# One core, linear attention with a router: padded DRAM blocks of x, evenly spaced steps of the second half, a split load of finished tiles and another order in the tail

## The chip, the cores and the metric

The kernel runs on one core of one Trainium2 chip. The metric is the device time of one execution in microseconds (us). The kernel before took 1077.23 us as the median of three runs (1074.14 to 1080.42).

## The reference, cut to what matters

`x` is four sequences of 512 rows and 512 columns. Each row is normalised (`xn`), and two branches read `xn`:

```
s = attention(xn)      # 16 heads of 128: q, k, v = silu(xn @ w_qkv); causal linear attention with a
                       # decay per head; RMS norm over all heads times norm_w; times
                       # sigmoid(xn @ w_gate); times w_out
g = silu(router(xn))   # softmax over 64 experts, the 8 largest kept:
                       # xn * sum(weights) + weights @ expert_bias
out = x + s * g
```

All arrays are float32.

## The kernel before, in words

**Halves and heads.** The four sequences are handled as two halves of two. For each half the kernel goes through 8 pairs of heads, so there are 16 cycles (`CYC`), numbered c. A cycle has 28 slots (`SLOTS`), one for each large matrix product, and the slot number is the clock of the whole plan: `plan(s, f, ...)` puts a step into slot s, and the main loop (L1261 to L1273) issues one product and then the steps of that slot (`inserts`). Every engine has one instruction list, filled in this order, and takes it in order; so a waiting instruction holds back all that stands behind it on its engine. Waits are on semaphores that name a finished instruction (`tk[...]`).

**Products.** One cycle has four groups g = 4c + k (weights of v, of k and q, of the gates, of k and q). A group is a product of two block matrices in a seven-product form (`PROD`), with each operand split in a high and a low part (`XH`, `XL`, `WH`, `WL`), so a product is six matmuls of 128x512 (L162 to L164). The seven blocks of x, X11 to XT4, lie in `XH` and `XL`, 512 KB each in either. The order within the loop is 6, 2, 5, 7 of g, then 1 of g + 1, then 4 and 3 of g. Products 1 and 2 write `BA`, 5 and 3 `BD`, the others `BS`. After each, ACT and DVE read the bank out (L536 to L595), and the next writer waits for that: `bd_free` is set by the add of L551.

**Second half of x.** It is prepared during cycles 4 to 7. For each of four tiles of rows (`x_second`, L986) SP loads two tiles into `XR` 0 and 1, statistics and a norm follow, and then two units (kk = 0, 1): `unit_turn` transposes four 128x128 pieces on PE into `PX` and ACT copies them to `U`, which lies in `XR` 2 and 3 (L1010); POOL, ACT and DVE make the differences and the two parts; `unit_store` (L1037) writes both to DRAM, `dxh` and `dxl`, and frees `U` when the store has landed. `PX` is also the bank of the output products (`ypart`, L775), which stand in slots 10, 12, ... 24 of each cycle, and of the router. While group 31 runs, the last of the first half, each of its products frees one block, and `x_block` (L1044), issued from ACT right behind that product, loads the block's second half from DRAM. The first product of group 32 that reads a block waits for its load (L509).

**Turned heads.** `v_turn` and `k_turn` transpose 32x32 squares on DVE into `VB` or `P`, and `v_move` and `k_move` (L616, four DMAs each, from SP) bring them to their partitions. `VB` is one buffer: the next `v_turn` waits until the move has landed (`vb_free`).

**Finished tiles.** At the start of the second half the first half's eight output tiles are finished: `final_load` (L1174) loads the tile of x and the router's part (`dgd`) into two of the four `XR` buffers, `final_first` multiplies on DVE (L964) and adds on POOL (L968), `final_store` stores from SP (L1187). For the second half the same is done in the tail (L1276 to L1320), straight from eight banks: `final_last` multiplies on DVE (L974), adds on POOL or DVE (L977) and stores from SP (L979). `rms_in` (L900) makes the row factors `rr`: eight matmuls (L905), one DVE instruction (L912), one on POOL (L914).

Of the kernel before, what the change touches and what calls it, by code (L numbers as in the profile page):

```python
# [5 lines left out]
F32 = mybir.dt.float32  # L6
# [6 lines left out]
T = 512  # L13
# [4 lines left out]
C = 128  # L18
# [7 lines left out]
EARLY = 8  # L26
NXT = 4


X11, X21, X22, XT3, XT1, XT2, XT4 = range(7)  # L30

# [6 lines left out]
def build(nc, x, wp, small, rw, eb, out):  # L38

    with ExitStack() as ctx:  # L40
# [6 lines left out]
        def sem(name):  # L47
            return ctx.enter_context(nc.semaphore(name))

        dxh = nc.dram_tensor("dxh", (128, 14, T), F32, kind="Internal").ap()  # L50
        dxl = nc.dram_tensor("dxl", (128, 14, T), F32, kind="Internal").ap()
        dgd = nc.dram_tensor("dgd", (NB, T, H), F32, kind="Internal").ap()

        XH = sb("XH", [128, 14, T], F32R)
# [50 lines left out]
        PT = pb("PT")  # L105
# [40 lines left out]
        def dma(s, f, e="sp"):  # L146

            count[s.name] += 16
            prog[e].append(lambda eng: f(eng).then_inc(s, 16))
            return s, count[s.name]  # L150

        def wait(e, *tokens):
            for t in tokens:
                if t and t[1] > waited[e].get(t[0].name, 0):
                    waited[e][t[0].name] = t[1]
                    prog[e].append(lambda eng, t=t: eng.wait_ge(t[0], t[1]))

        def f32(ap):
            return ap.bitcast(F32)
# [109 lines left out]
        def x_tile(b, t, *more):  # L269

            k = xr_next[0] % NXT
            xr_next[0] += 1
            wait("sp", xr_free[k], *more)
            return XR[:, k, :], dma(s_x[k], lambda e: e.dma_start(XR[:, k, :], x[b, t * 128:(t + 1) * 128, :])), k
# [692 lines left out]
            wait("pool", a, xtok)  # L967
            return op("pool", lambda e: e.tensor_tensor(xa, xa, ga, ALU.add))  # L968

        def final_last(b, t, bank, xt, gt, s, en):  # L970

            (xa, xtok), (ga, gtok) = xt, gt
            wait("dve", gtok, tk["rr", b], tk["yl", b, t])
            tk["y_read", b, t] = a = op("dve", lambda e: e.scalar_tensor_tensor(  # L974
                ga, bank[:, :], rr[:, b, t:t + 1], ga, ALU.mult, ALU.mult))
            wait(en, a, xtok)
            a = op(en, lambda e: e.tensor_tensor(xa, xa, ga, ALU.add))  # L977
            wait("sp", a)
            return dma(s, lambda e: e.dma_start(out[2 + b, t * 128:(t + 1) * 128, :], xa))  # L979
# [55 lines left out]
            tk["ul"] = op("dve", lambda e: e.tensor_tensor(U.bitcast(F32R), U, f32(UH), ALU.subtract))  # L1035

        def unit_store(t, kk):  # L1037
            s = slice(t * 128, (t + 1) * 128)
            wait("sp", tk["uh"], tk["ul"])
            dma(s_us, lambda e: e.dma_start(dxh[:, kk::2, s], f32(UH)))  # L1040
            d = dma(s_us, lambda e: e.dma_start(dxl[:, kk::2, s], U))
            xr_free[2] = xr_free[3] = tk["uh_free"] = tk["us"] = d

        def x_block(i, free):  # L1044
            s = slice(2 * i, 2 * i + 2)
            wait("act", tk["us"], free)
            dma(s_xb[i], lambda e: e.dma_start(f32(XH[:, s, :]), dxh[:, s, :]), "act")
            tk["xb", i] = dma(s_xb[i], lambda e: e.dma_start(f32(XL[:, s, :]), dxl[:, s, :]), "act")

# [2 lines left out]
        def plan(s, f, *a):  # L1054
            at.setdefault(s, []).append((f, a))
# [103 lines left out]
        plan(2, router_loads)  # L1159
        plan(17, router_parts, 0)  # L1160
        plan(8, router_parts, 1)
        for t, (load, stats, norm, s0, s1) in enumerate(((119, 122, 125, 129, 139), (140, 143, 146, 149, 159),
                                                         (160, 163, 166, 169, 179), (180, 183, 186, 189, 199))):
            plan(load, x_second, t)
            plan(stats, x_second_stats, t)
            plan(norm, x_second_norm, t)
            for kk, s in enumerate((s0, s1)):
                at.setdefault(s, []).insert(0, (unit_turn, (t, kk)))
                for i, f in ((1, unit_mix), (2, unit_more), (4, unit_high), (5, unit_low), (6, unit_store)):
                    plan(s + i, f, t, kk)  # L1170
# [1 line left out]
        fin = {}  # L1172

        def final_load(b, t):  # L1174
            xt = x_tile(b, t)
            k = xr_next[0] % NXT
            xr_next[0] += 1
            fin[b, t] = (*xt, XR[:, k, :], g_load(0, b, t, XR[:, k, :], s_gl[k], xr_free[k]), k)

        def final_first(b, t):  # L1180
            xa, xtok, k, ga, gtok, kg = fin[b, t]
# [8 lines left out]
        plan(base + 11, rms, 0)  # L1190
        plan(base + 15, rms, 1)
        for i, (b, t) in enumerate((b, t) for b in range(2) for t in range(4)):
            plan(base + (13 if i < 2 else 15) + 3 * i, final_load, b, t)
            plan(base + 18 + 3 * i, final_first, b, t)
            plan(base + 20 + 3 * i, final_store, b, t)


        t0 = [(G[:, t // 2, t % 2, :], dma(s_xs[t], lambda e, t=t: e.dma_start(
# [81 lines left out]
        tail_load(7, lambda: (*tk["q_read", 0], tk["p_read", 0]), ST[:, 0:T], P[:, 0, :])  # L1280
        banks = (PX, BS[0], BA, PS, BS[1], BD, PO, PX)
        ends = []

        def halves(r, b, ts):
            for t in ts:
                ypart_half(c, r, b, t, banks[4 * b + t])

        def finals(i, en):
            ends.append(final_last(*divmod(i, 4), banks[i], *tails[i], s_to[i], en))

        seed(1, 0, BS[1], tk["bs_free", 1])
        inter(c, 1, 1)
# [15 lines left out]
        finals(0, "pool")  # L1308
        seed(1, 3, PX, tk["y_read", 0, 0])
        finals(1, "dve")  # L1310
        finals(2, "pool")
        finals(3, "dve")
        halves(0, 1, (0,))
        rms_in(1, PT, 16, (tk["rr", 0],))
        halves(0, 1, (1, 2, 3))
        halves(1, 1, range(4))
        finals(4, "pool")
        finals(5, "dve")
        finals(6, "pool")
        finals(7, "dve")  # L1320
        assert not at, at.keys()
        wait("sp", *ends)
        for i in range(NXT):
# [74 lines left out]
```

How the kernel before makes its waits and increments, by code:

```python
        def op(e, f):  # L139
            s = done[e]
            count[s.name] += 1
            prog[e].append(lambda eng: f(eng).then_inc(s, 1))
            return s, count[s.name]
# [1 line left out]
        def dma(s, f, e="sp"):  # L146
            count[s.name] += 16
            prog[e].append(lambda eng: f(eng).then_inc(s, 16))
            return s, count[s.name]
# [1 line left out]
        def wait(e, *tokens):  # L152
            for t in tokens:
                if t and t[1] > waited[e].get(t[0].name, 0):
                    waited[e][t[0].name] = t[1]
                    prog[e].append(lambda eng, t=t: eng.wait_ge(t[0], t[1]))
```

## Time and profile before

| | |
|---|---|
| median of 3 runs | 1077.23 us |
| the profiled execution's own time | 1076.92 us |
| its span | 1075.2 us |
| PE / PEld / DVE / ACT / POOL busy | 97 / 83 / 59 / 56 / 63 % |
| mean granted clock of TensorE | 0.993 of full |
| DMA, mean over the span | 105 GB/s |

PE is TensorE, PEld its weight loads, DVE VectorE, ACT ScalarE, POOL GpSimd; SPq and ACTq are DMA issues of SyncE and ScalarE. The profile's times start at the span's start; the run's time is 1.7 us longer than the span. Line numbers are those of the kernel before. In the DMA views q1 is the queue of SP and q10 that of ACT, and a packet is one run of adjacent bytes.

### The profile page before, as it was taken

The numbers are of one execution on the slowest core, as the hardware profiler recorded it, in microseconds if no ns is written. First come the engines' busy times: TensorE is split into PE (matmuls) and PEld (weight loads), VectorE is DVE, ScalarE is ACT, GpSimd is POOL, SyncE is SP. The second block draws the span as 40 slices with busy tenths as digits, with TensorE's granted clock in tenths as the row PEclk, the third lists the DMA queues.
The fourth block names the chain that finished last, engine by engine and source line by source line (L and its number), as shares of the span: only waits on it lengthen the run. The fifth ranks groups of instructions, "written<-read, shape, count | busy, mean of one in ns | idle before, by whom it ended". The sixth has DMA issues, their size and how long they took to land.

```text
span 1075.2 us, 15318 instructions
## 1 busy us (share of the span) xinstructions
PE 1045.3 (97%) x5540; PEld 889.4 (83%) x5540; DVE 632.7 (59%) x1047; ACT 600.5 (56%) x1074; POOL 672.2 (63%) x700
## 2 busy tenths in 40 slices
PE   7899999999999999999899989999999999999997
PEld 6688887888888887888788878888888888888886
DVE  5357556664756665556355565756666575555557
ACT  7666556564656655575455445646556465645543
POOL 6966556574766857586566775755657375665613
PEclk8999999999999999999999999999999999999999
DMA  4233223252434435345733652321334251332235
GB/s 152 77 82 83 52 63 93 67 148 70 128 98 128 122 102 154 94 108 145 283 101 94 186 162 47 86 64 46 94 97 121 67 159 48 74 94 59 63 94 183
DMA packets 214508, 112.59 MB, mean 105 GB/s; under 512 B 175520, under 2 KB 189984, under 8 KB 214432
## 3 DMA queue, kind: packets, MB, share of 16 engines
q1 hardware_dynamic: 198880, 59.68, 23.5%
q10 hardware_dynamic: 15552, 51.93, 15.1%
q8 instruction: 44, 0.72, 0.3%
q14 instruction: 32, 0.26, 0.1%
HBM read 66.47 MB, written 15.73 MB: 76 GB/s over the span
## 4 chain that ended last, share of the span: by engine, by line
PE 85%; DMA 4%; POOL 3%; ACT 3%; DVE 2%; SPq 1%; issue 1%; ACTq 0%; DVEq 0%; POOLq 0%
PE BS L162 7%; PE BS L164 7%; PE BS L163 7%; PE PX L162 5%; PE PX L163 5%; PE PX L164 5%; PE PS L643 5%; PE BD L162 5%; PE PO L728 5%; PE BA L162 5%; PE BD L164 5%; PE BA L164 5%; PE BD L163 5%; PE BA L163 5%; PE PT L692 4%; PE PO L712 4%
## 5 line engine op out<-in xcount | busy, mean ns | idle before, releaser
L480 POOL TENSOR_TENSOR WL<-ST,WH 128x768 fp32r<-128x768 f32 (+1 forms) x128 | 172.5, 1349 | 131.4 <-ACT WH L476 131.2
L480 POOL TENSOR_TENSOR WL<-STG,WH 128x512 fp32r<-128x512 f32 (+1 forms) x128 | 133.2, 1041 | 139.6 <-ACT WH L476 139.6
L162 PE MATMUL BS<-XH,WH 128*128 128x512 f32 x384 | 159.2, 415 | 3.1 <-ACT K L560 1.6
L164 PE MATMUL BS<-XH,WL 128*128 128x512 f32 x384 | 150.7, 392 | 0.0
L163 PE MATMUL BS<-XL,WH 128*128 128x512 f32 x384 | 150.0, 391 | 0.0
L793 DVE TENSOR_TENSOR Y<-Y,PX 128x512 f32<-128x512 f32 x104 | 71.4, 687 | 122.5 <-PE PX L164 122.0
L162 PE MATMUL BD<-XH,WH 128*128 128x512 f32 x256 | 104.2, 407 | 5.5 <-DVE K L551 5.3
L751 POOL TENSOR_TENSOR SS<-SS,SQ 128x512 f32<-128x512 f32 x60 | 86.6, 1444 | 31.7 <-ACT SQ L743 31.7
L162 PE MATMUL BA<-XH,WH 128*128 128x512 f32 x256 | 102.9, 402 | 0.0
L164 PE MATMUL BD<-XH,WL 128*128 128x512 f32 x256 | 100.7, 393 | 0.0
L163 PE MATMUL BD<-XL,WH 128*128 128x512 f32 x256 | 100.4, 392 | 0.0
L164 PE MATMUL BA<-XH,WL 128*128 128x512 f32 x256 | 100.1, 391 | 0.0
L163 PE MATMUL BA<-XL,WH 128*128 128x512 f32 x256 | 99.8, 390 | 0.0
L162 PE MATMUL PX<-OH,GH 128*128 128x512 f32 x244 | 97.1, 398 | 2.5 <-ACT XR L1010 1.7
L476 ACT ACTIVATE WH<-ST 128x768 fp32r<-128x768 f32 (+1 forms) x128 | 80.1, 626 | 30.5 <-PE BD L164 15.4
L163 PE MATMUL PX<-OL,GH 128*128 128x512 f32 x244 | 95.1, 390 | 0.0
L164 PE MATMUL PX<-OH,GL 128*128 128x512 f32 x244 | 95.1, 390 | 0.0
L162 PEld LDWEIGHTS BS<-XH,WH 128*128 128x128 f32 x384 | 72.4, 189 | 17.5 <-ACT K L560 2.9
L536 ACT ACTIVATE BS<-BA 128x512 f32<-128x512 f32 x64 | 37.2, 582 | 88.2 <-PE BA L164 88.2
L164 PEld LDWEIGHTS BS<-XH,WL 128*128 128x128 f32 x384 | 72.0, 188 | 16.3
L163 PEld LDWEIGHTS BS<-XL,WH 128*128 128x128 f32 x384 | 72.5, 189 | 12.1
L611 DVE STREAM_TRANSPOSE VB<-VT 128x512 f32<-128x512 f32 x64 | 69.4, 1084 | 8.6 <-DMA V<-VB 8.4
(303 smaller groups left out, 2405.8 us busy)
## 6 DMA issues: line engine op xcount, KB each, us to landing
STG<-in_wp ACTq DMA_DIRECT2D x77, 512.0 KB, 3.8
V<-VB SPq DMA_DIRECT2D x248, 64.0 KB, 2.4
KN<-P SPq DMA_DIRECT2D x240, 48.0 KB, 2.1
XR<-in_x SPq DMA_DIRECT2D x38, 256.0 KB, 3.2
dgd<-XR ACTq DMA_DIRECT2D x16, 256.0 KB, 2.8
dxh<-WT SPq DMA_DIRECT2D x8, 448.0 KB, 3.4
dxl<-XR SPq DMA_DIRECT2D x8, 448.0 KB, 4.3
XH<-dxh ACTq DMA_DIRECT2D x7, 512.0 KB, 6.0
```

The source lines that it names most:

```text
L162: eng.matmul(o, ah, bh, start=first, stop=False, skip_group_check=skip)
L163: eng.matmul(o, ah, bl_, start=False, stop=False, skip_group_check=skip)
L164: return eng.matmul(o, al, bh, start=False, stop=last, skip_group_check=skip)
L476: a = op("act", lambda e, dst=dst, src=src: e.activation(WH[:, u, dst], src, ACT.Copy))
L480: a = op("pool", lambda e, dst=dst, src=src: e.tensor_tensor(WL[:, u, dst], src, f32(WH[:, u, dst]), ALU.subtract))
L611: return op("dve", lambda e: e.transpose(to.rearrange("p (q k j) -> p q k j", q=4, k=n), src.rearrange("p (k i q) -> p q k i", k=n, q=4)))
L643: m = e.matmul(PS[:, chunk(k)], kk[:, chunk(k)], q[:, chunk(k)], start=(k == 0), stop=True, skip_group_check=True)
L692: m = e.matmul(PT[:, chunk(i)], KD[:, chunk(i)], v[:, i, :], start=True, stop=True)
L712: m = e.matmul(PO[:, chunk(k)], KV[:, k - 1, :], q[:, chunk(k)], start=(k == 1), stop=False, skip_group_check=True)
L728: m = e.matmul(PO[:, chunk(k)], v[:, k, :], P[:, b, chunk(k)], start=False, stop=True, skip_group_check=True)
L751: a = op("pool", lambda e: e.tensor_tensor(SS[:, b, :], SS[:, b, :], SQ[:, :], ALU.add))
L793: a = op("dve", lambda e: e.tensor_tensor(dst, dst, bank[:, :], ALU.add))
```

## The change

Four things are changed. `dxh` and `dxl` get a dimension of four tiles with 16 unused floats behind each 128, so that the 512 columns of a block are no longer adjacent in DRAM and `x_block` reads them as runs of 512 bytes; the stores write the same runs as before, at other addresses. The units of the second half start in slots 129 + 11n (n = 0 to 7) rather than 129, 139, 149, 159, 169, 179, 189, 199; their loads come 22 slots apart. For finished tiles the load of the router's part is issued 4 slots ahead of the multiply and the load of x 2 slots ahead, in place of both together 3 ahead (5 for the first two), and every second tile starts one slot later. In the tail the second row factor is computed ahead of the multiplies of tiles 2 and 3, the sum of tile 5 moves from DVE to POOL, that of tile 6 from POOL to DVE, and the sums of 6 and 7 come behind both multiplies.

```diff
--- before.py
+++ after.py
@@ -26,6 +26,8 @@
 EARLY = 8
 NXT = 4
 
+RUN = 16
+
 
 X11, X21, X22, XT3, XT1, XT2, XT4 = range(7)
 
@@ -47,8 +49,8 @@
         def sem(name):
             return ctx.enter_context(nc.semaphore(name))
 
-        dxh = nc.dram_tensor("dxh", (128, 14, T), F32, kind="Internal").ap()
-        dxl = nc.dram_tensor("dxl", (128, 14, T), F32, kind="Internal").ap()
+        dxh = nc.dram_tensor("dxh", (128, 14, 4, C + RUN), F32, kind="Internal").ap()
+        dxl = nc.dram_tensor("dxl", (128, 14, 4, C + RUN), F32, kind="Internal").ap()
         dgd = nc.dram_tensor("dgd", (NB, T, H), F32, kind="Internal").ap()
 
         XH = sb("XH", [128, 14, T], F32R)
@@ -967,12 +969,16 @@
             wait("pool", a, xtok)
             return op("pool", lambda e: e.tensor_tensor(xa, xa, ga, ALU.add))
 
-        def final_last(b, t, bank, xt, gt, s, en):
+        def final_last(b, t, bank, xt, gt, s):
 
             (xa, xtok), (ga, gtok) = xt, gt
             wait("dve", gtok, tk["rr", b], tk["yl", b, t])
             tk["y_read", b, t] = a = op("dve", lambda e: e.scalar_tensor_tensor(
                 ga, bank[:, :], rr[:, b, t:t + 1], ga, ALU.mult, ALU.mult))
+            return a, xa, ga, xtok, s
+
+        def final_sum(b, t, part, en):
+            a, xa, ga, xtok, s = part
             wait(en, a, xtok)
             a = op(en, lambda e: e.tensor_tensor(xa, xa, ga, ALU.add))
             wait("sp", a)
@@ -1035,17 +1041,18 @@
             tk["ul"] = op("dve", lambda e: e.tensor_tensor(U.bitcast(F32R), U, f32(UH), ALU.subtract))
 
         def unit_store(t, kk):
-            s = slice(t * 128, (t + 1) * 128)
             wait("sp", tk["uh"], tk["ul"])
-            dma(s_us, lambda e: e.dma_start(dxh[:, kk::2, s], f32(UH)))
-            d = dma(s_us, lambda e: e.dma_start(dxl[:, kk::2, s], U))
+            dma(s_us, lambda e: e.dma_start(dxh[:, kk::2, t, 0:C], f32(UH)))
+            d = dma(s_us, lambda e: e.dma_start(dxl[:, kk::2, t, 0:C], U))
             xr_free[2] = xr_free[3] = tk["uh_free"] = tk["us"] = d
 
         def x_block(i, free):
+            wait("act", tk["us"], free)
             s = slice(2 * i, 2 * i + 2)
-            wait("act", tk["us"], free)
-            dma(s_xb[i], lambda e: e.dma_start(f32(XH[:, s, :]), dxh[:, s, :]), "act")
-            tk["xb", i] = dma(s_xb[i], lambda e: e.dma_start(f32(XL[:, s, :]), dxl[:, s, :]), "act")
+            for to, src in ((XH, dxh), (XL, dxl)):
+                tk["xb", i] = dma(s_xb[i], lambda e, to=to, src=src: e.dma_start(
+                    f32(to[:, s, :]).rearrange("p s (t n) -> p s t n", t=4),
+                    src[:, s, :, 0:C]), "act")
 
 
 
@@ -1159,8 +1166,8 @@
         plan(2, router_loads)
         plan(17, router_parts, 0)
         plan(8, router_parts, 1)
-        for t, (load, stats, norm, s0, s1) in enumerate(((119, 122, 125, 129, 139), (140, 143, 146, 149, 159),
-                                                         (160, 163, 166, 169, 179), (180, 183, 186, 189, 199))):
+        for t in range(4):
+            load, stats, norm, s0, s1 = (22 * t + s for s in (119, 122, 125, 129, 140))
             plan(load, x_second, t)
             plan(stats, x_second_stats, t)
             plan(norm, x_second_norm, t)
@@ -1172,10 +1179,17 @@
         fin = {}
 
         def final_load(b, t):
-            xt = x_tile(b, t)
-            k = xr_next[0] % NXT
-            xr_next[0] += 1
-            fin[b, t] = (*xt, XR[:, k, :], g_load(0, b, t, XR[:, k, :], s_gl[k], xr_free[k]), k)
+
+            kx = xr_next[0] % NXT
+            kg = kx + 1
+            fin[b, t] = [kx, XR[:, kg, :], g_load(0, b, t, XR[:, kg, :], s_gl[kg], xr_free[kg]), kg]
+            xr_next[0] += 2
+
+        def final_x(b, t):
+            f = fin[b, t]
+            k = f[0]
+            wait("sp", xr_free[k])
+            f[0:1] = [XR[:, k, :], dma(s_x[k], lambda e: e.dma_start(XR[:, k, :], x[b, t * 128:(t + 1) * 128, :])), k]
 
         def final_first(b, t):
             xa, xtok, k, ga, gtok, kg = fin[b, t]
@@ -1190,9 +1204,11 @@
         plan(base + 11, rms, 0)
         plan(base + 15, rms, 1)
         for i, (b, t) in enumerate((b, t) for b in range(2) for t in range(4)):
-            plan(base + (13 if i < 2 else 15) + 3 * i, final_load, b, t)
-            plan(base + 18 + 3 * i, final_first, b, t)
-            plan(base + 20 + 3 * i, final_store, b, t)
+            s = base + 18 + 3 * i + i // 2
+            plan(s - 4, final_load, b, t)
+            plan(s - 2, final_x, b, t)
+            plan(s, final_first, b, t)
+            plan(s + 2, final_store, b, t)
 
 
         t0 = [(G[:, t // 2, t % 2, :], dma(s_xs[t], lambda e, t=t: e.dma_start(
@@ -1280,13 +1296,19 @@
         tail_load(7, lambda: (*tk["q_read", 0], tk["p_read", 0]), ST[:, 0:T], P[:, 0, :])
         banks = (PX, BS[0], BA, PS, BS[1], BD, PO, PX)
         ends = []
+        parts = {}
 
         def halves(r, b, ts):
             for t in ts:
                 ypart_half(c, r, b, t, banks[4 * b + t])
 
         def finals(i, en):
-            ends.append(final_last(*divmod(i, 4), banks[i], *tails[i], s_to[i], en))
+            parts[i] = final_last(*divmod(i, 4), banks[i], *tails[i], s_to[i])
+            if en:
+                sums(i, en)
+
+        def sums(i, en):
+            ends.append(final_sum(*divmod(i, 4), parts[i], en))
 
         seed(1, 0, BS[1], tk["bs_free", 1])
         inter(c, 1, 1)
@@ -1308,16 +1330,18 @@
         finals(0, "pool")
         seed(1, 3, PX, tk["y_read", 0, 0])
         finals(1, "dve")
+        halves(0, 1, (0,))
+        rms_in(1, PT, 16, (tk["rr", 0],))
         finals(2, "pool")
         finals(3, "dve")
-        halves(0, 1, (0,))
-        rms_in(1, PT, 16, (tk["rr", 0],))
         halves(0, 1, (1, 2, 3))
         halves(1, 1, range(4))
         finals(4, "pool")
-        finals(5, "dve")
-        finals(6, "pool")
-        finals(7, "dve")
+        finals(5, "pool")
+        finals(6, None)
+        finals(7, None)
+        sums(6, "dve")
+        sums(7, "dve")
         assert not at, at.keys()
         wait("sp", *ends)
         for i in range(NXT):
```

## Rows read from the trace of the kernel before

**Rows 1.** The page's engine line; PE is TensorE matmul

```profile
PE 1045.3 (97%) x5540; PEld 889.4 (83%) x5540; DVE 632.7 (59%) x1047; ACT 600.5 (56%) x1074; POOL 672.2 (63%) x700
```

**Rows 2.** Waits of PE, whole run: us in total, times, longest us

```profile
PE BD L162 <- DVE K L551: 5.3, 1, 5.3
PE PO L712 <- DVE KV L700: 2.1, 1, 2.1
PE PX L162 <- ACT XR L1010: 1.7, 1, 1.7
...
PE PT L692 <- ACT KD L680: 1.5, 2, 0.8
...
PE PX L162 <- DVE Y L790: 0.8, 1, 0.8
```

**Rows 3.** Chain that ended last, 515 to 545: start us, us, what

```profile
520.77 15.87 DMA V<-VB
...
536.67 1.08 DVE VB L611
```

**Rows 4.** Timeline of PE, 538 to 548: start us, us, instruction, idle before

```profile
538.46 0.77 PE L162 MATMUL BD<-XH,WH 128*128 128x512 f32 x1 [5.33 <-DVE K L551]
...
541.16 1.11 PE L643 MATMUL PS<-Q,K 128*128 128x128 f32 x8
...
542.70 0.48 PE L162 MATMUL BS<-XH,WH 128*128 128x512 f32 x1
...
546.12 0.48 PE L162 MATMUL BS<-XH,WH 128*128 128x512 f32 x1
...
547.60 0.40 PE L162 MATMUL BD<-XH,WH 128*128 128x512 f32 x1
```

**Rows 5.** Busy time by window; the last numbers are PEclk, DMA share, GB/s

```profile
538.00:541.20 3.20, 2.74 (x7) 2.19 (x8) 1.82 (x3) 2.65 (x5) 0.12 (x1) 0.50 0.53 111
```

**Rows 6.** DMA engines' busy tenths in 40 slices of 516 to 540

```profile
DMA  0000468999999999999999999999999999998236
```

**Rows 7.** DMA queues, 527 to 532: packets, MB, share of 16 engines

```profile
q10 hardware_dynamic: 565, 2.06, 101.1%
q1 hardware_dynamic: 121, 0.01, 1.9%
```

**Rows 8.** DMA queue and a landing, 350.5 to 355: stores in 512 B runs

```profile
q1 hardware_dynamic: 1824, 0.92, 71.0%
...
dxh<-WT SPq DMA_DIRECT2D x1, 448.0 KB, 3.3
```

**Rows 9.** DMA queue, 303 to 308 (a move of V, runs of 128 B)

```profile
q1 hardware_dynamic: 2256, 0.31, 35.9%
```

**Rows 10.** DMA queue, 363 to 367 (a move of K, runs of 384 B)

```profile
q1 hardware_dynamic: 576, 0.20, 20.9%
```

**Rows 11.** Timeline, 422 to 431: a store's issue; the copy behind its landing

```profile
422.85 1.70 SPq L1041 DMA_DIRECT2D dxl<-XR  x1
...
429.91 0.60 ACT L1010 ACTIVATE XR<-PX 128x512 f32<-128x512 f32 x1 [1.70 <-DMA dxl<-XR]
```

**Rows 12.** Chain, 1050 to 1076: start us, us, what

```profile
1050.16 0.89 PE PO L728 x8
```

**Rows 13.** Chain and timeline, 610 to 618: a finished tile

```profile
610.63 3.42 DMA out<-XR
...
617.78 1.02 DVE L964 SCALAR_TENSOR_TENSOR XR<-Y,rr,XR 128x512 f32<-128x512 f32 x1 [5.73 <-DMA XR<-dgd]
```

**Rows 14.** Timeline, 1061 to 1073: PE and DVE in the tail

```profile
1061.62 0.95 PE L905 MATMUL PT<-TINY,SS 128*128 128x4 f32 x8
...
1066.01 0.15 DVE L912 TENSOR_SCALAR TINY<-PT 128x4 f32<-128x4 f32 x1
...
1067.35 0.75 DVE L974 SCALAR_TENSOR_TENSOR STG<-BS,rr,STG 128x512 f32<-128x512 f32 x1 [1.19 <-issue]
...
1071.35 1.20 DVE L977 TENSOR_TENSOR ST<-ST,P 128x512 f32<-128x512 f32 x1
```

## Prediction

> **What bounds the kernel now.** I read the page first, then PE's waits, then the chain and the timeline where the waits are long, and last the DMA views of those stretches. The page says that TensorE is the bound: it is busy 97% of the span [rows 1], every product follows the one before, and no other engine is over 83%. A change that leaves the matmuls as they are, as this one does, can only win what PE loses by waiting. The list of PE's waits [rows 2] shows how little that is outside the start: 5.3 us once at the crossing to the second half, 2.1 and 0.8 us at the finished tiles, 1.7 us and about 0.8 us at the units. To that comes the tail, where PE has ended and other engines finish. Together some 12 us of 1077, and the four parts of the change are each aimed at one of these.
>
> The long wait must be read with care, since the name in it is not its cause. The chain [rows 3] goes through a move of V that took 15.87 us to land. `v_turn` stands on DVE for the one buffer `VB`, and the add that frees `BD` stands behind it; the product on `BD` starts 5.33 us late [rows 4]. [...] Its six matmuls take 2.70 us (538.46 to 541.16), where the product from 546.12 to 547.60 takes 1.48 [rows 4]. So the wait costs 5.3 + 1.2 = 6.5 us in all.
>
> Why did the move take so long? The 16 DMA engines are full from about 518.5 to 538.2 [rows 6], with the blocks of x. In the middle of it ACT's queue gets 101% and SP's 1.9% [rows 7]: 565 packets of mostly 4096 bytes against 121 small ones. On an engine with both queues filled, each 128-byte packet of V waits for a 4096-byte packet of x to pass. A few engines that are far behind hold back the whole move.
>
> **Part 1, runs of 512 bytes, and what they cost.** A block of x (high and low part, 1.05 MB) is now 2048 packets, 128 for each engine. The gain is sure in its direction: a packet of V then waits for an eighth of the bytes, the move of V lands in some 6 us, and the wait of [rows 4] for DVE goes. What is late next is the data itself. The trace before has no DRAM read in 512-byte runs. The nearest row is the units' stores: 0.92 MB in 71.0% of 4.5 us on 16 engines [rows 8] is 18.0 GB/s for an engine, so 3.64 us a block. The reads of today move 2.06 MB in 101.1% of 5 us [rows 7], 25.5 GB/s, 2.57 us a block. Each block gets 1.07 us longer.
>
> Now the queue's work, counted before and after. The move of V is 2048 packets of 12.7 ns (35.9% of 5 us on 16 engines over 2256, [rows 9]), 1.63 us; that of K 512 packets of 23.2 ns [rows 10], 0.74 us; a load of weights is half a block, 1.29 us. The first block (X11) is loaded long before. Six blocks, one load of weights, one V and one K are 6 x 2.57 + 1.29 + 1.63 + 0.74 = 19.1 us before; it ended at 538.2 [rows 6], so it began in effect at 519.1. After: 6 x 3.64 + 1.29 + 0.74 + 2 x 1.63 (the next move of V, which waited for the first, falls into the stretch now) = 27.1 us, to 546.2. A landing adds 1.7 us at its two ends (3.3 less 56 packets of 28 ns, [rows 8]), of which I put 1.0 behind the data: 547.2. The last block, X22, is needed by the product that begins at 547.60 today; less the 6.5 us it is 541.1. It comes 6.1 us late. Most of that shows earlier: XT3 lands at 540.0 for a product due at 542.70 - 6.5 = 536.2, 3.8 us late. So the wait for V is exchanged for waits for x of 6.1 us together, in two or three pieces. Whether the clock falls again is open, as 3.8 us is shorter than 5.3; I take half of 1.2. Net: 6.1 + 0.6 - 6.5 = +0.2 us. Bounds: if the runs of 512 bytes go at today's rate nothing is late, -6.5; at the bytes a nanosecond of K's packets (16.6 GB/s for an engine, 3.95 us a block) and with the full slow clock, +2.6. I take the stores' row, as it has the same run length.
>
> [...]
>
> [...] The DRAM gaps only move the stores' addresses: nothing.
>
> **Part 2, steps 11 apart.** `U` is freed by the landing of the store issued 6 slots behind the turn. With 10 slots between turns four remain for it, and ACT stood 1.70 us for such a landing [rows 11], PE behind it; with 11 there are five. That removes the 1.7 us and the late `KD` of 0.8 us [rows 2]: -2.5. But the turns now fall at slots 162, 184 and 206, which are 22, 16 and 10 of their cycles, where an output product stands that needs the same bank `PX`. None did so before: all eight old slots fell between. The output product must wait for ACT's copy: 0.20 us to start, 0.60 for the copy [rows 11], 0.05 back, with up to 0.6 for an eviction ahead of it; 0.85 to 1.45 us each. At 206 the step `intra` stands between and covers it with 0.89 us of matmuls [rows 12]. I take 1.0 for each of the two others: +2.0. Net -0.5, between -2.5 and +1.5. The last store moves from slot 205 to 211 + 1, two products ahead of the first `x_block`, so ACT may stand there for its landing with its evictions queued behind; the next product of that group is three products away, and this cover pays for up to some 2 us. Without it the evictions would hold PE for as long as ACT stood.
>
> **Part 3, finished tiles.** Today SP waits for the store of the tile before last (3.42 us), then loads x and the router's part together, and DVE stands 5.73 us for the latter [rows 13], with `KV` behind it: that is PE's 2.1 us, and 0.8 us for `Y` comes from the next [rows 2]. With the router's part issued four slots ahead, ahead of the wait for the store, DVE finds it there: -2.9. The load of x has two slots, some 5 us, for a transfer like the store's 3.42; behind a move of K on SP it can be late, and then POOL stands. I take +0.3 for that. Net -2.6, between -2.9 and 0.
>
> **Part 4, tail.** The matmuls for the second factor begin at 1061.62, but DVE gets to `TINY` only at 1066.01, behind two multiplies and a sum, and then idles 1.19 us for POOL's `rr` [rows 14]. In the new order `TINY` runs at about 1063.5 and `rr` is made under the multiplies of tiles 2 and 3. DVE keeps four sums and eight multiplies, so its last sum (1071.35, 1.20 us) ends 1.2 us earlier, and the last store with it. Next late is DVE's own work. Net -1.2, between -1.2 and 0.
>
> **Sum.** 0.2 - 0.5 - 2.6 - 1.2 = -4.1 us on the profiled execution's 1076.9: **1072.8 us**. That execution is 0.3 us under the median of the runs, which lets me compare with either.
>
> **Rivals.** (a) *The runs of 512 bytes cost nothing.* Then V's wait and the slow clock go and no block is late: a further -6.7, 1066.1 us. For it: the long wait is DVE's for V and no block is late today. Against it: 18.0 against 25.5 GB/s. [...] Chance 0.2.
>
> (b) *ACT gets stuck issuing the loads.* By 525 four blocks are issued, 512 packets for an engine, of which at 28 ns only some 200 have gone; today the same blocks are 64 packets. [...] The point from which it decides is a depth under 300 packets: ACT then holds its seed and evictions until the queue drains, up to 541, and its 6 us of work follow. PE would be near 13 us late in place of 6.1, with slow clocks: 1072.8 + 8 = 1081 us, slower than before. Against it: SP issued a move of K at its usual pace while V's was pending. Chance 0.12.
>
> (c) *The small waits come back elsewhere.* `PX` costs 1.45 us thrice, ACT's wait in slot 214 reaches PE, and POOL's wait for x eats the gain of part 3: about +4, 1077 us, no change. For it: ACT and POOL work only a slot or two ahead of PE. Chance 0.18.
>
> **How the numbers follow.** Forecast 0.5, (a) 0.2, (b) 0.12, (c) 0.18. A measurement of this kernel can tell about 0.5% from no change, that is 1071.8 and 1082.6. Faster: all of (a) and a third of the forecast's case, 0.36. Slower: half of (b), a fifth of (c) and a bit of the forecast's upper end, 0.11. The rest, 0.53, is within. The range must hold (a) and (c) and the unknown rate: 1065.5 to 1079.5; outside lie most of (b) and the outer ends.
>
> **What would show it.** In the changed profile: the move of V at the crossing lands in under 8 us and PE's wait there names a DMA into `XH` or `XL`, not DVE; ACT's queue moves x at 280 to 290 GB/s; DMA is full to about 546. `Y` and `KV` no longer hold PE at the finished tiles; two new waits of about 1 us for ACT's copy of `PX` (`XR`, L1010's successor) stand at slots 162 and 184. In the tail `TINY` comes ahead of the multiplies. The prediction is wrong if the crossing has no wait (rate), if ACT's issues take over 1 us (b), or if the total moves by more than the 5 us that I give the parts.

## The result and the profile after

The changed kernel takes 1075.13 us (median of 20 runs, 1072.71 to 1077.81), the kernel before 1077.28 us (20 runs). The ratio is 0.9977, with a 95% interval of 0.9967 to 0.9988: some 2.5 us faster, within the half per cent that I called no change. The forecast was 1072.8. The profiled execution took 1074.73 us with a span of 1073.0, 2.2 us under that of before.

The page and the list of PE's waits of the changed kernel (us in total, times, longest) show what took the place of [rows 1, 2]. All lines have moved, by 2 up to about 970 and by 6 behind: L645 is the former L643, L546 the former L544, L682 the former L680, L1016 the former L1010, and L1053 is the load of a block.

```profile
span 1073.0 us, 15320 instructions
...
PE 1047.7 (98%) x5540; PEld 891.9 (83%) x5540; DVE 632.2 (59%) x1047; ACT 601.1 (56%) x1074; POOL 673.0 (63%) x700
```

```profile
PE PX L164 <- ACT XR L1016: 4.0, 2, 2.8
PE BS L164 <- ACT Q L546: 3.4, 1, 3.4
PE PT L694 <- ACT KD L682: 2.1, 2, 1.3
```

Outside the start, DVE is gone from the list: both its wait for V and its waits at the finished tiles. ACT has come instead: its copy of `PX` holds PE for 4.0 us in place of 1.7, its `KD` for 2.1 in place of 1.5, and its read-out of `BS` for 3.4 in place of nothing.

**Where the time went.** The order of the score matmuls is the same in both kernels, so the start of one and the same group shows how far the second kernel is behind. First before, then after (timeline of PE; start us, us):

```profile
373.91 1.05 PE L643 MATMUL PS<-Q,K 128*128 128x128 f32 x8
...
503.39 1.05 PE L643 MATMUL PS<-Q,K 128*128 128x128 f32 x8
...
514.77 1.06 PE L643 MATMUL PS<-Q,K 128*128 128x128 f32 x8
...
574.06 1.05 PE L643 MATMUL PS<-Q,K 128*128 128x128 f32 x8
...
640.83 1.05 PE L643 MATMUL PS<-Q,K 128*128 128x128 f32 x8
```

```profile
373.99 1.05 PE L645 MATMUL PS<-Q,K 128*128 128x128 f32 x8
...
506.23 1.05 PE L645 MATMUL PS<-Q,K 128*128 128x128 f32 x8
...
517.99 1.06 PE L645 MATMUL PS<-Q,K 128*128 128x128 f32 x8
...
578.33 1.05 PE L645 MATMUL PS<-Q,K 128*128 128x128 f32 x8
...
640.22 1.05 PE L645 MATMUL PS<-Q,K 128*128 128x128 f32 x8
```

The drift is +0.1 us before the units, +2.8 behind them, +3.2 at the group of 514.77, +4.3 at the group of 574.06, -0.6 behind the finished tiles, and it stays there to the tail, where the rest of the 2.2 us comes. I count the crossing from the group of 514.77 to that of 574.06. So the units lose about 3 us, the crossing 1.1 (0.8 of it a wait for `KD` behind the load of X11, see below), the finished tiles win 4.9, the tail 1.6.

**The crossing.** The chain no longer goes through a move of V. The timeline of ACT's DMA issues shows the new wait (start us, us):

```profile
523.58 0.79 ACTq L1053 DMA_DIRECT2D XH<-dxh  x1
...
524.40 1.59 ACTq L1053 DMA_DIRECT2D XL<-dxl  x1
...
528.09 2.36 ACTq L1053 DMA_DIRECT2D XL<-dxl  x1
...
530.49 1.96 ACTq L447 DMA_DIRECT2D STG<-in_wp  x1
...
532.97 1.75 ACTq L1053 DMA_DIRECT2D XL<-dxl  x1
534.77 0.60 ACT L546 ACTIVATE Q<-BS 128x512 f32<-128x512 f32 x1 [6.86 <-issue]
```

Before, the same issues took 0.33 to 0.65 us, and the load of weights (`STG`) 0.75. ACT stands 6.86 us in its own issues, four of them with nothing between, with the read-out of `BS` behind them, and PE waits 3.4 us for that. This is the wait of my rival (b). How full the queue was can be counted: by 530.45 ACT had issued six half-blocks of 1024 packets since 522, and the DMA view of ACT's queue from 522 to 530.45 gives the packets moved (packets, MB, share):

```profile
q10 hardware_dynamic: 3452, 1.74, 79.1%
```

With one closing packet for each DMA and engine ([rows 8] count 1824 packets for two stores of 896, 32 more) these are 6240; 6240 - 3452 leaves 174 packets for each of 16 engines at the moment the long issue ended. The same count at the ends of the other long issues of blocks (526.0, 534.7, 543.2) gives 165 to 167. That would fit a queue that holds some 170 for an engine and an issue that lasts until there is room; this is my inference from the counts, no view shows the depth. It does not fit the load of weights in the list: it adds only 9 packets for an engine, took 1.96 us, and the same count at its end (532.45) gives 117. Nor does it fit the store of before that took 1.70 us to issue [rows 11]: of the 3936 packets that SP issued from 419.37 to 424.55, 2442 had moved by then (DMA view), which leaves 93 for an engine. What those two issues waited for stays open. The rate is what the forecast needed: in the view from 531 to 534 the queues, nearly all of it ACT's, move

```profile
DMA packets 1769, 0.86 MB, mean 288 GB/s; under 512 B 96, under 2 KB 1769, under 8 KB 1769
```

288 GB/s, against 417 in runs of 4096 bytes (the same view of the kernel before, 527 to 532, where [rows 7] are from).

**The units.** The second PX wait, from the timeline of the changed kernel:

```profile
434.37 0.58 SPq L1045 DMA_DIRECT2D dxh<-WT  x1
...
435.00 0.68 SPq L1046 DMA_DIRECT2D dxl<-XR  x1
...
439.65 0.60 ACT L1016 ACTIVATE XR<-PX 128x512 f32<-128x512 f32 x1 [2.76 <-DMA dxl<-XR]
...
440.31 0.79 PE L164 MATMUL PX<-OH,GH 128*128 128x512 f32 x1 [2.75 <-ACT XR L1016]
```

The store of slot 179 went out only at 434.4, since a move of V stood ahead of it on SP from 430.8. It landed at 439.6; until then `U` was not free, ACT could not copy `PX`, and the output product in the same slot 184 had no product between to cover it. The granted clock of 425 to 450 is 0.93, 1.00 before. The other wait, at slot 162, is 1.26 us, as priced.

The old spacing had the same fault. The landing that held ACT for 1.70 us before [rows 11] was that of the store of slot 175, which also stood behind a move of V (timeline of SP, before):

```profile
419.37 2.74 SPq L616 DMA_DIRECT2D V<-VB  x4
422.21 0.59 SPq L1040 DMA_DIRECT2D dxh<-WT  x1
```

The last store of a unit, now issued from 510.7 on, held ACT ahead of the load of X11: ACT stood 6.06 us up to 516.96, that load's two issues included, and PE waited 0.80 us for `KD` up to 519.84.

**The tail.** Timeline of DVE, the answer to [rows 14]:

```profile
1062.82 0.15 DVE L914 TENSOR_SCALAR TINY<-PT 128x4 f32<-128x4 f32 x1
...
1065.80 0.74 DVE L976 SCALAR_TENSOR_TENSOR STG<-BS,rr,STG 128x512 f32<-128x512 f32 x1
...
1068.43 1.23 DVE L983 TENSOR_TENSOR STG<-STG 128x512 f32<-128x512 f32 x1
1069.58 0.68 DVE L983 TENSOR_TENSOR ST<-ST,P 128x512 f32<-128x512 f32 x1
```

From `TINY` on no idle time is left, and the last sum takes 0.68 us in place of 1.20. The 1.20 us was not DVE's own time. In both kernels an add on DVE that ran beside an add on POOL ended 0.54 to 0.56 us behind POOL's, whenever it had started (seven adds, 1.20 to 1.55 us long). Before, POOL's last add ended at 1071.99 and DVE's at 1072.55; after, POOL was done at 1069.11, ahead of DVE's last add (timeline of POOL, first before, then after):

```profile
1070.73 1.26 POOL L977 TENSOR_TENSOR STG<-STG 128x512 f32<-128x512 f32 x1 [1.29 <-DVE STG L974]
...
1066.62 2.49 POOL L983 TENSOR_TENSOR STG<-STG 128x512 f32<-128x512 f32 x2 [1.29 <-DVE STG L976]
```

### The profile page after: what moved, and what is told of

Read it like the earlier page. It is cut to its first block, busy times and chain, and to the rows that moved or that the text cites. A ratio compares the mean times of both kernels' runs of the same rounds, so it can differ in the third digit from the quotient of the medians.

```text
span 1073.0 us, 15320 instructions
## 1 busy us (share of the span) xinstructions
PE 1047.7 (98%) x5540; PEld 891.9 (83%) x5540; DVE 632.2 (59%) x1047; ACT 601.1 (56%) x1074; POOL 673.0 (63%) x700
## 4 chain that ended last, share of the span: by engine, by line
PE 88%; ACT 4%; POOL 3%; DMA 2%; DVE 1%; ACTq 1%; issue 1%; SPq 1%; DVEq 0%; POOLq 0%
PE BS L164 8%; PE BS L166 8%; PE BS L165 8%; PE BA L164 5%; PE BA L166 5%; PE BA L165 5%; PE PX L164 5%; PE BD L164 5%; PE BD L166 5%; PE PO L730 5%; PE BD L165 5%; PE PS L645 5%; PE PX L166 5%; PE PX L165 5%; PE PT L694 4%; PE PO L714 4%
```

## The experiments

Each was timed beside the kernel before on the same chip (the last four kernels on another chip than the eight ahead of them). Ratios are to before, with 95% intervals; drifts are those of the profiled execution at the groups that stand at 503.4, 574.1 and 640.8 in the trace of before.

**The four parts alone.** Each kernel is the kernel before with one part of the diff above.

> The kernel before with part 1 alone (gaps in DRAM, blocks read in runs of 512 bytes). Theory A (the four parts act each in its own place, as the drift between the two traces reads): the crossing costs about 1 us more than before, 5.3 + 1.2 us of wait and slow clock being exchanged for ACT standing in its own DMA issues (issues of up to 2.4 us) and PE behind it; in all +0.5 to +1.5 us, at most 'same'. Rival B (part 1 is good and was spoilt by part 2, whose last store lands only when ACT wants to load X11): without part 2 the crossing is 1 to 3 us cheaper than before, -1 to -3 us, and no ACT issue is over 1 us.

> The kernel before with part 2 alone (units 11 slots apart). Theory A: +3 us, all lost between 380 and 520 us: PE waits about 1.3 and 2.8 us for ACT's copy of PX at slots 162 and 184, where an output product shares the slot and the bank. Rival B: the waits of 0.8 and 1.7 us that the old spacing had go and the new ones are 1 us each, so the sum is -0.5 us, and the longer wait in the trace of after is chance (a store that lands late beside other transfers).

> The kernel before with part 3 alone (the router's part of finished tiles first). Theory A: -4.5 to -5 us between 590 and 640, PE has no wait there at all. Rival B: only PE's listed waits of 2.1 and 0.8 us go, -2.6 to -3 us, and the rest of what the drift shows there belonged to the crossing's backlog that part 1 leaves behind.

> The kernel before with part 4 alone (tail order). Theory A: -1.6 us, all behind the last matmul: 1.2 us for DVE's idle wait on rr and 0.5 us because the last sum on DVE has no sum on POOL beside it (0.68 in place of 1.20 us). Rival B: only the 1.2 us, if the last sum still takes 1.2 us.

| part alone | median us | ratio | interval | drift at 503 / 574 / 641 |
|---|---|---|---|---|
| 1, gaps | 1078.44 | 1.0013 | 1.0000 to 1.0027 | +0.8 / +0.8 / +1.4 |
| 2, steps | 1080.11 | 1.0024 | 1.0011 to 1.0036 | +2.3 / +3.6 / +3.9 |
| 3, finished tiles | 1072.35 | 0.9958 | 0.9944 to 0.9972 | -0.5 / +0.4 / -4.5 |
| 4, tail | 1076.44 | 0.9993 | 0.9979 to 1.0006 | +1.4 / +0.6 / +1.0 |

The drift of a part where it changes nothing tells how far one execution differs from another: about 1 us. Over the crossing, where they are the kernel before, the kernels with part 3 and part 4 alone drift by +0.9 and -0.9. The medians carry the verdict. Part 3 wins 4.5 us and part 2 loses 2.6 us, both as theory A had it, though the wait at slot 184 is 1.9 us in the kernel with part 2 alone and not 2.8. Part 1 loses 1.4 us or nothing, and its drift over the crossing is 0.0; rival B falls, since ACT's issues take up to 2.30 us without part 2 as well and PE waits for the same read-out. From its waits of PE:

```profile
PE BS L164 <- ACT Q L546: 3.5, 1, 3.5
```

Part 4 is not clear by its timing. In its trace the drift goes from +1.0 at 641 to -0.6 at the end, 1.6 us. The idle wait of 1.19 us is gone, and its last sum on DVE is short, as in the whole change:

```profile
1070.07 1.22 DVE L981 TENSOR_TENSOR STG<-STG 128x512 f32<-128x512 f32 x1
1071.21 0.68 DVE L981 TENSOR_TENSOR ST<-ST,P 128x512 f32<-128x512 f32 x1
```

So theory A, 1.2 us for the wait and 0.5 for the sum, fits the trace, and rival B falls. The product of the four ratios is 0.9988, the whole change 0.9977, at the edge of its interval: the parts about add up.

**Part 1 undone within the change.**

```diff
-        dxh = nc.dram_tensor("dxh", (128, 14, 4, C + RUN), F32, kind="Internal").ap()
+        dxh = nc.dram_tensor("dxh", (128, 14, T), F32, kind="Internal").ap()
...
-            dma(s_us, lambda e: e.dma_start(dxh[:, kk::2, t, 0:C], f32(UH)))
+            dma(s_us, lambda e: e.dma_start(dxh[:, kk::2, s], f32(UH)))
```

> The changed kernel with part 1 undone (blocks adjacent in DRAM again, 4096-byte runs; parts 2 to 4 kept). Theory A (part 1 is worth about nothing, as it only exchanges DVE's wait for V against ACT standing in its issues): the time stays within 1.5 us of the changed kernel, 0.9965 to 0.999 of before; PE's wait of about 5 us behind DVE's add on BD comes back and ACT's issues of blocks fall to under 0.7 us. Rival B (part 1 alone measured slower only because of the wait for X11's store): undoing it now costs 2 us or more, 0.999 to 1.001 of before.

It takes 1074.18 us, 0.9957 (0.9945 to 0.9969), 2 us less than the changed kernel if the ratios are compared, 1 us by the medians; the ratio lies just below theory A's range. ACT's issues of blocks are at 0.33 to 0.51 us again. DVE's wait is back, and slow clock behind it (0.86 in the window of 525 to 550):

```profile
PE BD L164 <- DVE K L553: 4.8, 1, 4.8
```

The drift over the crossing is +1.2 us, and +1.1 in the changed kernel, so that +1.1 is not part 1's. Rival B falls: part 1 wins nothing in company either, and may cost 1 to 2 us. The two long waits are worth about the same.

**Runs of 1024 bytes.**

```diff
-        dxh = nc.dram_tensor("dxh", (128, 14, 4, C + RUN), F32, kind="Internal").ap()
+        dxh = nc.dram_tensor("dxh", (128, 14, 2, 2 * C + 16), F32, kind="Internal").ap()
...
-                    f32(to[:, s, :]).rearrange("p s (t n) -> p s t n", t=4),
-                    src[:, s, :, 0:C]), "act")
+                    f32(to[:, s, :]).rearrange("p s (t n) -> p s t n", t=2),
+                    src[:, s, :, 0:2 * C]), "act")
```

> The changed kernel with runs of 1024 bytes (two tiles adjacent, a gap after each pair). Theory Q (ACT stands because its queue holds some 150 to 165 packets for each DMA engine, the count found whenever one of its long issues ended): a block is 64 packets an engine in place of 128, so ACT's issues fall to under 1 us each, V's move lands in about 8 us, and the crossing gets 2 to 4 us cheaper than in the changed kernel: 0.994 to 0.996 of before. Rival D (the crossing is bound by the data, 6 blocks and the rest filling the DMA engines): the rate rises from about 290 to 350 GB/s and the wait moves from ACT to the landing of a block; 1 to 2 us cheaper, 0.996 to 0.997.

It takes 1073.04 us, 0.9957 (0.9939 to 0.9974). ACT's issues are shorter, but not all under 1 us; from its timeline:

```profile
529.57 0.54 ACTq L445 DMA_DIRECT2D STG<-in_wp  x1
530.15 0.47 ACTq L1052 DMA_DIRECT2D XH<-dxh  x1
530.64 1.36 ACTq L1052 DMA_DIRECT2D XL<-dxl  x1
...
536.32 1.55 ACTq L1052 DMA_DIRECT2D XH<-dxh  x1
537.90 1.42 ACTq L1052 DMA_DIRECT2D XL<-dxl  x1
```

The count at 537.87 and 539.3 gives 141 and 142 packets an engine, so the bound is nearer to one of packets (141 against some 170) than of bytes (144 KB against 87 KB an engine). The DMA view of 532 to 535 has 332 GB/s. V's move lands in 7.1 us. The drift over the crossing is -0.8 us, 1.9 less than in the changed kernel, though crossings of the same code differ by as much. What is late now is neither ACT's queue nor a block: PE's longest wait is for `KD`, which waits for a move of K.

```profile
PE PT L692 <- ACT KD L680: 4.0, 2, 3.6
```

Theory Q holds for the mechanism, but the issues did not all fall under 1 us, and the gain is at its lower end and the upper end of rival D's. By its interval the kernel is not clear of the changed one.

**Runs aligned to 256 bytes.**

```diff
-RUN = 16
+RUN = 64
```

> The changed kernel with 64 unused floats behind each run in place of 16, so that each 512-byte run starts at a multiple of 256 bytes. In the changed kernel the reads of blocks move 280 to 295 GB/s where the stores of before had 285 with aligned runs, and a packet takes some 32 ns, not 28. Theory L (unaligned starts cost a packet 3 to 4 ns): reads rise to about 300 to 320 GB/s, the crossing gets 0.5 to 1.5 us cheaper, 0.996 to 0.998 of before. Rival N (reads of 512 bytes are simply that fast): rates and time stay as they are, 0.9967 to 0.9988.

1074.27 us, 0.9965 (0.9953 to 0.9978), which overlaps the changed kernel; the time alone would suit either theory. In the view from 537 to 540, between the same two issues, the queue moves 293 GB/s, and 301 in the changed kernel; from 531 to 534 it is 291 against 288. Theory L falls by these rates: the start of a run does not matter here.

```profile
DMA packets 1732, 0.88 MB, mean 293 GB/s; under 512 B 31, under 2 KB 1731, under 8 KB 1731
```

**No unit in a slot with an output product.**

```diff
-        for t in range(4):
-            load, stats, norm, s0, s1 = (22 * t + s for s in (119, 122, 125, 129, 140))
+        for t, (load, stats, norm, s0, s1) in enumerate(((119, 122, 125, 129, 140), (141, 144, 147, 151, 161),
+                                                         (162, 165, 168, 173, 183), (184, 187, 190, 195, 205))):
```

> The changed kernel with the units at slots 129, 140, 151, 161, 173, 183, 195, 205 in place of 129 + 11n: no unit shares a slot with an output product. Theory A: PE's two waits for ACT's copy of PX (1.3 and 2.8 us) go, 3 us less than the changed kernel, 0.9945 to 0.9955 of before. Rival B (the long wait is for the landing of U's store, which still comes whenever one is late): at most 1 us less, 0.9965 to 0.998, the wait showing up at another turn.

Both were wrong: 1078.14 us, 1.0005 (0.9993 to 1.0018), 3 us slower than the changed kernel. The drift behind the units is +6.7 us. One wait for `PX` of 2.6 us is left; the others became waits for `KD`, for instance (timeline; PE stands 3.3 us for the `KD` behind it)

```profile
404.83 1.17 POOL L289 TENSOR_TENSOR rs<-ve,TINY 128x2 f32<-128x2 f32 x1
...
406.68 1.52 ACT L305 ACTIVATE XR<-XR,TINY,rs 128x512 f32<-128x512 f32 x2 [2.98 <-POOL TINY L294]
```

The third tile's norm came one slot earlier than in the changed kernel, where POOL was still full with weights and squares; ACT stood for its row factors. Sharing a slot is not the only cost: every step of a unit meets a queue.

**The stores ahead of the moves.**

```diff
-                for i, f in ((1, unit_mix), (2, unit_more), (4, unit_high), (5, unit_low), (6, unit_store)):
+                for i, f in ((1, unit_mix), (2, unit_more), (4, unit_high), (5, unit_low)):
                     plan(s + i, f, t, kk)
+                at.setdefault(s + 6, []).insert(0, (unit_store, (t, kk)))
```

> The changed kernel with the units' stores put at the front of their slot, ahead of a move of V or K in the same slot. In the trace of the changed kernel the store of slot 179 was issued only behind a move of V, landed at 439.6 and held ACT's copy of PX for 2.76 us and PE for 2.75. Theory S (the order on SP's queue is what makes the units cost): that wait goes and the drift over the units falls from +3.0 to 0 to +1 us, 0.995 to 0.9965 of before. Rival B (the turns lose by sharing slots and PX whatever SP does): less than 1 us better, 0.997 to 0.9985, or V's move is now late and DVE or PE waits for it.

On the chip of this kernel and the next three the kernel before ran at 1079.82 us (11 runs, 1075.56 to 1084.53), some 2 us above its other medians, so the ratios of these four look better than they should, and the four are best compared with one another and by their traces. This one takes 1071.44 us, 0.9922 (0.9902 to 0.9942), below the ranges of both theories; by the medians it is 3.7 us under the changed kernel, by the profiled spans 3.2. The same turn as above, from its timeline:

```profile
430.94 0.55 SPq L1045 DMA_DIRECT2D dxh<-WT  x1
431.53 0.68 SPq L1046 DMA_DIRECT2D dxl<-XR  x1
432.25 4.50 SPq L618 DMA_DIRECT2D V<-VB  x4
...
437.86 0.60 ACT L1016 ACTIVATE XR<-PX 128x512 f32<-128x512 f32 x1 [0.81 <-DMA dxl<-XR]
...
438.51 0.50 PE L164 MATMUL PX<-OH,GH 128*128 128x512 f32 x1 [0.79 <-ACT XR L1016]
```

The store leaves 3.4 us earlier, PE waits 0.79 in place of 2.75 us, the clock stays at 1.00, and the drift at 503 is -0.4, not +2.8. Theory S holds: most of what the units lost was the place of the store on SP's queue. The other wait at slot 162 stays, 1.3 us.

**Parts 3 and 4 with other blocks.** `s2` is the kernel before with parts 3 and 4; `s3` has the 1024-byte runs besides; `s4` also the stores first, at the old slots.

> Parts 3 and 4 alone (parts 1 and 2 undone). If the parts add up: 0.9958 x 0.9993 = 0.9951 of before, some 5 us, 2.5 us better than the whole change, 0.994 to 0.996. Rival (the drift in the finished tiles was so large only because parts 1 and 2 had put PE behind): 0.9965 to 0.9975.

> Parts 3 and 4, and runs of 1024 bytes at the old slots. Theory Q (with 64 packets a block ACT's issues hardly stand, and the last store is not in the way of the load of X11 at the old slots): the crossing costs 2 to 4 us less than before, 0.991 to 0.9935 of before. Rival D (the wait is only moved to the data): at most 1 us less than parts 3 and 4 alone, 0.994 to 0.9955.

> The same with the units' stores at the front of their slots. Theory S: PE's waits of 0.8 and 1.7 us at the units of the old slots go as well (the long landing of 7 us stood behind a move of V in slot 175), 1 to 2.5 us less than without, 0.989 to 0.992 of before. Rival: the moves of V and K that now stand behind the stores hold DVE, no difference within 0.5 us.

| kernel | median us | ratio | interval | drift at 503 / 574 / 641 |
|---|---|---|---|---|
| parts 3, 4 | 1071.19 | 0.9917 | 0.9895 to 0.9940 | +0.5 / +1.3 / -3.6 |
| + 1024 bytes | 1072.02 | 0.9928 | 0.9906 to 0.9950 | +1.4 / +1.3 / -3.6 |
| + stores first | 1067.51 | 0.9886 | 0.9865 to 0.9907 | -1.5 / -4.6 / -9.4 |

Parts 3 and 4 alone are as fast as the whole change with its stores mended, so parts 1 and 2 can go. The ratio of `s2` lies below both ranges, for the reason given above; its profiled span is 5.2 us under that of before, which is what the parts add up to. The 1024-byte runs at the old slots win nothing that shows: the ratio of `s3` alone falls in theory Q's range, but `s2` without these runs is as low, and the medians are the same within their spread. The stores first win 4.5 us by the medians, with a ratio just below theory S's range. In the traces 2.9 us of that is at the units, where the waits of 1.6, 1.1 and 1.2 us of `s3` shrink to one of 1.1. Another 2.9 us is at the crossing, where `s3` and `s4` have the same wait for `KD`,

```profile
PE PT L692 <- ACT KD L680: 4.6, 2, 3.5
```

but the clock fell behind it in `s3` (0.86 over 525 to 550, 0.50 in 540 to 545) and not in `s4` (1.00). Whether the clock falls after such a wait was not the same from kernel to kernel. It fell also behind much shorter waits: at slot 184 behind 1.8 us (part 1 undone), 1.9 (part 2 alone) and 2.2 (aligned runs), where it is 0.83, 0.83 and 0.84 over 440 to 450, but not behind 2.2 us with part 1 alone or 2.1 in `s2`, both about 430 us in (1.00 over 425 to 450). I did not find what decides it. `s4` is the fastest kernel of the study, about 12 us under the kernel before by the medians beside it and 11 by the spans.

## Why the prediction was right or wrong

The total was forecast at -4.1 us and came out at -2.5; time, range and the case of no change hold. Two of the four terms are well off, in opposite directions, and a third was met for another reason than the one given.

**What bounds the kernel** held. PE's waits [rows 2], with the clock behind them, and the tail are what moved, and the matmuls are the same.

**Part 1, +0.2 us.** Part 1 alone measured +1.4 us (0 to +2.9). The traces don't put that at the crossing: it is 0.0 there with part 1 alone, and the +1.1 of the whole change is +1.2 with part 1 undone. V's move lands in 6.3 us and no longer holds DVE, and the exchange is about even. That a packet of V waits behind a packet of x is seen in the trace of before: over 529 to 532 SP's queue moved 15, 14 and 14 packets a microsecond, all of V, and ACT's 110, 108 and 117, which is 7 for each of 16 engines, so the figures fit two engines that take the queues in turn while the others had none of V left. The move took 15.9 us beside packets of 4096 bytes, 7.1 beside 1024 and 6.3 beside 512. The step "What is late next is the data itself" was wrong. The rate was right (18.0 GB/s an engine is 288 GB/s for 16), but no wait of PE names a block. ACT stood first, in the issues, as rival (b) said; because it stood, the later blocks were also asked for later. One of the prediction's own signs of being wrong, issues of ACT over 1 us, thus came true, and that the term was met is luck. Rival (b) had the mechanism and its place. Its price was wrong: it put PE 13 us behind, and PE waited 3.4 + 1.3 us. An issue let ACT go again after 1.6 to 2.4 us each time, and ACT got to its work between the first of them; only from 528.1 to 534.7 did four follow without a break. The slow clock came in full, not by half (0.93 over 525 to 550, as before, where it was 0.50 from 538.0 to 541.2 [rows 5] and 1.00 from 525 to 538; 0.63 us a matmul in place of 0.39 from 535.4 to 538.8).

The stores' row [rows 8] was the right one to take: the reads ran at 288 GB/s, at which a 512-byte packet takes 28 ns of an engine, as there. Against 417 GB/s in runs of 4096 bytes this puts (a) out.

**Part 2, -0.5 us.** It measured +2.6 us alone (+1.2 to +3.9), and the trace of the whole has +3.2 at 514.77, with another 0.8 behind the load of X11. The failed step is "I take 1.0 for each of the two others": the wait at slot 162 was 1.26, inside the bounds (before, a copy that nothing held began at 358.20, 0.28 us behind the next product's start, and PE began 0.05 us behind the copy of [rows 11]), but that at slot 184 was 2.75 with a slow clock behind it. I had priced the shared bank and the landing of `U`'s store apart, and taken the landing as settled by the fifth slot. It was not, since the store stood behind a move of V in slot 179, as the one of slot 175 had before. The spacing was not what made that landing late, the place on SP's queue was; and with product and turn in one slot, nothing lies between ACT's wait and PE's. The experiment with the stores first took 2 us off that wait, and a slow clock with it. The upper bound of +1.5 was too low for the same reason. The load of X11 did stand for the last store, as feared: ACT issued it at 515.9 and PE then waited 0.8 us for `KD`, which I had costed at nothing. Taking the units out of the slots of the output products, without touching the order on SP, did not help (3 us slower), so the shared slot is not the main cause.

**Part 3, -2.6 us.** It measured -4.5 us alone and -4.9 in the trace, and PE has no wait left in 575 to 650. The mechanism was right and the term mis-sized. I counted two of PE's waits, 2.1 and 0.8 us, and left out one of 0.8 us for `KD` in the same stretch [rows 2], and the +0.3 did not come (POOL stood 1.4 us for x once, PE not at all). These make 3.7 us. The rest of the 4.9 is in no listed wait, but the starts of PE's matmuls place it: 0.8 us directly around the three waits, as the first matmuls behind a wait take longer (0.94 us in place of 0.83 for six of 128x128), and 0.4 between 609.3 and 613.1, where a product on `BD` starts a little late.

**Part 4, -1.2 us.** Its own timing can't tell (0.9993, 0.9979 to 1.0006); both traces with it end 1.6 us better than their drift. The idle 1.19 us is gone as forecast. The term left out that the last sum would no longer run beside one on POOL: it is 0.5 us shorter in both traces. Together 1.7 us; the other changes in the tail nearly cancel.

**Rivals.** (b) happened in mechanism, and at the price of the forecast. SP's move of K, named against it, was indeed issued in 2.49 us at 528.81 beside 2.51 at 541.71, but SP's queue held only some 80 packets of V then (2112 issued, 2030 moved by 529). (c), small waits that come back elsewhere, happened at the units and cost 3 us; part 3's surplus paid for most of it. That the sum came near is thus in part luck: -0.5 became about +3 and -2.6 about -4.7. Of the other signs, DMA stayed full to about 551, not 546 (a load of weights issued at 545.6 is in that), and `Y` and `KV` no longer hold PE.

## What to carry to other kernels

Moving a step past another on a queue changes when its transfer lands: before a spacing is called long enough, list what stands ahead of the transfer on its issuing queue in that very slot, and check that the waiting reader does not share its slot with the bound engine's next user of the bank. Cutting long DRAM reads into short runs freed the other queue here (V's move landed in 6.3 us in place of 15.9), but it paid twice, in rate (288 in place of 417 GB/s) and in the packets that the issuer's queue must take (issues of 1.6 to 2.4 us); if the issuer is also a computing engine, count packets per DMA engine. Where PE's waits are listed for a stretch, add up all of them, whatever engine they name, before a term is sized.

## What the runs showed of the hardware that I had not expected

DMA issues of blocks on ACT took 0.33 to 0.65 us before. With 512-byte packets they lasted 1.6 to 2.4 us when 165 to 174 packets for each DMA engine were outstanding at their end (the others 0.37 to 1.18), and 1.4 to 1.6 us with 1024-byte packets at about 141. A load of weights of 9 large packets an engine stood 1.96 us among them and ended at 117, and before, a store's issue on SP took 1.70 us and ended at 93, so the rule of these queues is not known. Reads of 512 bytes from DRAM ran at 288 to 301 GB/s, as the stores did (288 GB/s by [rows 8]: 18.0 GB/s for each engine), of 1024 bytes at 332, and of 4096 at 417. Starts at multiples of 64 or of 256 bytes made no difference (301 and 293 GB/s). An add of 128x512 on DVE with both inputs in SBUF took 0.68 us where POOL had finished, and beside an add on POOL it ended 0.54 to 0.56 us behind POOL's, whenever it had started.
